# Pivot statistics, output in two halves and another order of work in a cross-attention kernel with a group norm

## What is computed

```
q, k = Wq y + bq, Wk y + bk          # 128 x 1024 each
scores = q k^T / sqrt(128)           # per head, 16 x 16, summed over 1024 positions
attn   = softmax(scores)
o      = Wo (attn (Wv x + bv)) + bo + x
mu, var = mean(o), var(o)            # over all 128 x 1024 values of the batch
out    = (o - mu) * rsqrt(var + 1e-5) * gn_w + gn_b
```

## Time and profile before

| | |
|---|---|
| median of 3 runs | 174.3 us (174.11 to 174.43) |
| the profiled execution | 174.09 us, its span 172.3 us |
| mean granted clock of PE | 0.982 of full speed |
| busy share of the span | PE 94%, DVE 88%, ACT 79%, POOL 65% |
| DMA | 50.8 MB, mean 295 GB/s |

### The profile page before, as it was taken

How to read it: one execution, slowest core, us unless ns; L and a number is a source line. 1 busy time by engine, 2 the same in 40 slices (tenths; PEclk the granted TensorE clock), 3 DMA queues, 4 the chain that set the end, 5 groups by cost and what they waited for, 6 DMA issues and landing times. The chain is left out here.

```text
span 172.3 us, 3697 instructions
## 1 busy us (share of the span) xinstructions
PE 161.3 (94%) x997; PEld 128.1 (74%) x997; DVE 150.8 (88%) x555; ACT 136.7 (79%) x356; POOL 112.5 (65%) x166
## 2 busy tenths in 40 slices
PE   7989999999999999999999999999999999999720
PEld 7777888777777788887777777888877777776410
DVE  1796999999999999999999999999999999977541
ACT  3656588988888888889888888888899888776342
POOL 3287677778777777777787777777777787731010
PEclk9999999999999999999999999999999999999975
DMA  5999778899989999999989999899999865633233
GB/s 198 416 402 372 261 226 305 331 339 327 334 331 345 364 318 332 310 338 335 331 312 338 343 352 359 307 327 337 327 336 332 297 234 230 246 123 124 122 122 122
DMA packets 14276, 50.83 MB, mean 295 GB/s; under 512 B 1712, under 2 KB 1712, under 8 KB 14256
## 3 DMA queue, kind: packets, MB, share of 16 engines
q1 hardware_dynamic: 13968, 50.34, 80.4%
q10 hardware_dynamic: 288, 0.27, 0.5%
HBM read 33.82 MB, written 16.78 MB: 294 GB/s over the span
## 5 line engine op out<-in xcount | busy, mean ns | idle before, releaser
L509 PE MATMUL o_ps<-x_sb,m_sb 128*128 128x512 f32 x128 | 63.0, 614 | 0.0
L426 DVE TENSOR_TENSOR hl_sb<-y_sb,hl_sb 128x512 fp32r<-128x512 f32 x64 | 47.1, 737 | 0.8 <-ACT hl_sb L321 0.8
L266 POOL TENSOR_TENSOR rstd<-veps,nhalf 128x1 f32<-128x1 f32 x32 | 28.3, 885 | 23.2 <-DVE veps L431 23.2
L321 ACT CAST hl_sb<-y_sb 128x512 fp32r<-128x512 f32 x64 | 39.6, 622 | 1.9 <-DMA y_sb<-in_ctx_dram 1.9
L509 PE MATMUL g_ps<-hl_sb 128*128 128x258 f32 x256 | 38.6, 293 | 0.0
L361 ACT ACTIVATE out_sb<-o_ps,shift,gain 128x1024 f32<-128x1024 f32 (+1 forms) x32 | 38.3, 1198 | 0.1
L295 POOL TENSOR_TENSOR lsuma<-hl_sb 128x256 f32<-128x256 f32 x31 | 23.2, 749 | 22.8 <-DVE hl_sb L426 22.8
L509 PEld LDWEIGHTS o_ps<-x_sb,m_sb 128*128 128x128 f32 x128 | 21.8, 191 | 14.8 <-issue 14.8
L509 PEld LDWEIGHTS g_ps<-hl_sb 128*128 128x128 f32 x256 | 32.8, 190 | 0.0
L457 DVE BATCH_NORM_STATS2 bn<-o_ps 128x6 f32<-128x512 f32 x32 | 22.4, 699 | 4.1 <-PE o_ps L509 0.5
L316 ACT ACTIVATE a_sb<-sc_sb,smin 128x128 f32<-128x128 f32 x32 | 12.9, 403 | 16.0 <-DVE smin L417 15.9
(11 more groups left out here) (64 smaller groups left out, 297.8 us busy)
## 6 DMA issues: line engine op xcount, KB each, us to landing
y_sb<-in_ctx_dram SPq DMA_DIRECT2D x32, 512.0 KB, 5.0
x_sb<-in_x_dram SPq DMA_DIRECT2D x32, 512.0 KB, 5.4
out_dram<-out_sb SPq DMA_DIRECT2D x31, 512.0 KB, 4.8
out_dram<-out_sb SPq DMA_DIRECT2D x2, 256.0 KB, 2.2
w_in<-in_weights_dram ACTq DMA_DIRECT2D x1, 256.0 KB, 5.7
cols<-in_columns_dram ACTq DMA_DIRECT2D x1, 3.0 KB, 3.4
```

Of the source, the lines that this page charges most:

```text
L266: nc.gpsimd.tensor_tensor(rstd[:, h1:h1 + 1], veps[:, h1:h1 + 1], nhalf[:, :], ALU.pow).then_inc(rstd_ready, 1)
L321: nc.scalar.copy(hl_sb[:, k, chunks, 0:C], y_sb[:, k, chunks, :]).then_inc(h_ready, 1)
L426: nc.vector.tensor_tensor(hl_sb[:, ky, chunks, C:2 * C], y_sb[:, ky, chunks, :], hl_sb[:, ky, chunks, 0:C].bitcast(F32), ALU.subtract).the ...
L509: return nc.tensor.matmul(dst, lhsT, rhs, start=start, stop=stop, **more)
```

## The change

The pipeline keeps its lags, and nearly every instruction stays. What differs:

- Statistics: the mean with the bias is no longer formed before the product. A pivot (x's first column times the row sums of `m_sb`, plus the bias column; `pivot_column`) is averaged by PE one step ahead, and `shift_by_pivot` gives `cp`. Then the row deviation (`deviation`) and its square plus the variance (`square`) go with the next batch's pivot through one product of three columns (`statistics`), which stands between the two o products and behind the query product of the next step. `negative_variance` and `variance` follow on DVE, then POOL's power as before.
- `fold_matrix` also accumulates the row sums, and the bias column is an instruction of its own.
- PE waits for both halves of the rest before the Gram product starts (in effect one piece).
- The output is written in two halves on ACT, with the copy of the cross product between them.
- Rounding (`round_half`) is one batch ahead: ACT rounds batch t + 1 in step t, and DVE's rests are both of batch t.
- `EARLY` is 2: PE sums the rests of batches 0 and 1 itself, after the transpose. Small matrices get two buffers each. The last batch's o goes to other PSUM banks, and its two halves are stored from ACT and SP.

```diff
+            for t in range(B + LAGS + 1):                 # PE
+                input_product(t - 4, 0)
+                query(t - 2)
+                statistics(t - 5)
+                input_product(t - 4, 1)
+                softmax_product(t - 3)
+                gram(t - 1, 0)
+                gram(t - 1, 1)
+                value_product(t - 3)
+                scores(t - 2)
+                transpose_cross(t - 1)
...
+            for t in range(-1, B + LAGS):                 # ACT
+                normalise(t - 3)
+                round_half(t + 1, 0)
+                scale_bk(t - 2)
+                copy_r(t - 3)
+                gain_and_shift(t - 5)
+                output(t - 5, 0)
+                copy_cross(t - 1)
+                output(t - 5, 1)
+                exponential(t - 2)
+                round_half(t + 1, 1)
...
+            for t in range(B + LAGS + 1):                 # DVE
+                copy_sum(t - 2)
+                invert_sum(t - 3)
...
+                rest_half(t, 0)
+                negative_variance(t - 5)
+                shift_by_pivot(t - 4)
+                variance(t - 5)
+                weighted_shift(t - 5)
+                rest_half(t, 1)
...
+                statistics_of(t - 4, 0)
+                add_query_bias(t - 2)
+                statistics_of(t - 4, 1)
+                fold_matrix(t - 3)
+                aggregate(t - 4)
+                minimum(t - 2)
+                deviation(t - 4)
+                add_gram(t - 1)
+                pivot_column(t - 3)
+                square(t - 4)
...
+            for t in range(B + LAGS):                     # POOL
+                inverse_deviation(t - 5)
+                fold_first(t)
+                fold_last(t - 1)
+                fold_second(t)
+                fold_sum(t)
...
+            def negative_variance(b):
+                dve.wait_ge(st_ready, b + 2)
+                nc.vector.tensor_scalar(nvar[:, b % 2:b % 2 + 1], st_ps[:, 0:1], st_ps[:, 0:1], st_ps[:, 1:2],
+                                        ALU.mult, ALU.add).then_inc(nvar_ready, 1)
+            def variance(b):
+                dve.wait_ge(nvar_ready, b + 1)
+                nc.vector.tensor_scalar(veps[:, b % 2:b % 2 + 1], nvar[:, b % 2:b % 2 + 1], -1.0, EPS,
+                                        ALU.mult, ALU.add).then_inc(veps_ready, 1)
+            def gain_and_shift(b):
+                act.wait_ge(rstd_ready, b + 1)
+                nc.scalar.mul(gain[:, b % 2:b % 2 + 1], gn_w, rstd[:, b % 2:b % 2 + 1])
+                act.wait_ge(wshift_ready, b + 1)
+                nc.scalar.activation(shift[:, b % 2:b % 2 + 1], wshift[:, b % 2:b % 2 + 1], ACT.Identity,
+                                     bias=gn_b, scale=rstd[:, b % 2:b % 2 + 1]).then_inc(affine_ready, 1)
+            def copy_cross(b):
+                act.wait_ge(hl_ready, b + 1)
+                nc.scalar.copy(b2_sb[:, b % 2, :], g_ps[:, C:2 * C]).then_inc(b2_copied, 1)
+            def transpose_cross(b):
+                pe.wait_ge(b2_copied, b + 1)
+                transposed = product(g_ps[:, 0:C], b2_sb[:, b % 2, :], ident_r[:, :], start=False, skip_group_check=True)
+            def statistics(b):
+                if live(b):
+                    pe.wait_ge(q_ready, b + 1)
+                if live(b + 1):
+                    pe.wait_ge(pivot_ready, b + 2)
+                if live(b) or live(b + 1):
+                    part = slice(0 if live(b) else 2, 3 if live(b + 1) else 2)
+                    product(st_ps[:, part], onesn[:, :], st_in[:, b % 2, part]).then_inc(st_ready, 1)
```

More of the change, by code:

```diff
@@ L205, in _ @@
         def _(sp):
[L206 to L220, removed]
-                if is_step(t, LAST):
-                    ko = (k - 5) % UNROLL
-                    for half, done in ((0, normed), (1, normed_dve)):
-                        part = slice(half * HALF, (half + 1) * HALF)
-                        sp.wait_ge(done, B if half == 0 else 1)
-                        sp.dma_start(batch(out, B - 1)[:, part], out_sb[:, ko, part]).then_inc(out_done[ko], 16)
-                elif has(t, 5):
-                    ko = (k - 5) % UNROLL
-                    sp.wait_ge(normed, t - 4)
-                    sp.dma_start(batch(out, t - 5), out_sb[:, ko, :]).then_inc(out_done[ko], 16)
@@ L239, in _ @@
+            for b in range(SLOTS):
+                load_y(b)
+            for t in range(B + LAGS):
+                if t >= 1:
+                    load_y(t + SLOTS - 1)
+                load_x(t)
+                store(t - 5)
+            for k in range(SLOTS):
+                sp.wait_ge(out_done[k], 16 * (B // SLOTS + (k == LAST % SLOTS)))
         @block.gpsimd
@@ new lines, in output @@
+            def output(b, half):
+                if not live(b) or b == LAST and half == 1:
+                    return
+                if b >= SLOTS and half == 0:
+                    act.wait_ge(out_done[b % SLOTS], loads(b - SLOTS))
+                if b == LAST:
+                    act.wait_ge(affine_dve, 1)
+                else:
+                    act.wait_ge(affine_ready, b + 1)
+                k = 2 if b == LAST else b % 2
+                nc.scalar.activation(out_sb[:, b % SLOTS, half_of(half)], o_half(b, half), ACT.Identity,
+                                     bias=shift[:, k:k + 1], scale=gain[:, k:k + 1]).then_inc(normed, 1)
+                if b == LAST:
+                    act.wait_ge(normed, 2 * LAST + 1)
+                    act.dma_start(batch(out, b)[:, half_of(0)], out_sb[:, b % SLOTS, half_of(0)]).then_inc(out_done[b % SLOTS], 16)
@@ L515, in keep_busy, with gram @@
                     product(o_ps[:, 1, 0:P], onesn[:, :], onesn[:, :])
+            def gram(b, half):
+                if not live(b):
+                    return
+                pe.wait_ge(l_ready, 2 * b + 1 + half)
+                if half == 0 and b >= 1:
+                    pe.wait_ge(g_copied, b)
+                    pe.wait_ge(s_copied, b)
+                for c in range(half * HCH, (half + 1) * HCH):
+                    mm = product(g_ps[:, 0:HL], hl_sb[:, b % SLOTS, c, 0:C], hl_sb[:, b % SLOTS, c, :],
+                                 start=(c == 0), stop=(c == CH - 1))
+                if half == 1:
+                    mm.then_inc(hl_ready, 1)
```

659 lines of the change are left out of this document (348 added, 311 removed).

## The result

The changed kernel takes 189.5 us (median of 4 runs, 188.1 to 191.6) against 174.2 us (4 runs, 174.1 to 174.4): 1.085 times as long, 95% interval 1.078 to 1.092. The profiled execution took 190.07 us with a span of 188.0 (before 174.09 and 172.3).

What follows compares the result with a forecast made beforehand. PE set the old 4.74 us step; a ring through power, output, copy and transpose was to make it 5.02. 28 x 0.28 = +7.8, then - 0.1 + 0.4 - 0.6 = +7.5: 181.8 us, range 174.8 to 185.0.

Steps and rivals of the forecast that it cites:

- Is an engine longer than the ring?: Check of each engine's work per step: PE 4.50, ACT 4.59, DVE 4.64 us, POOL unchanged, all below the ring's 5.02.
- the forecast ring: Repeated steps: statistics product, DVE pair, power, gain, shift, first output half, copy, transpose, next o product; 5.02 us a step.
- The start: Up to the first o products of step 4: +0.4 us, bounds -0.3 to +1.9.
- step 4: The step before the ring runs, with no output and set by DVE: about -0.1 us.
- Step 32: Last of the 28 steps in which the ring was to run: +0.28 us.
- The end: Steps 33 and 34 and the last two stores: -0.6 us.
- (1): Rival: the ring is real but shorter, negative_variance 0.16 and power 0.93, step 4.79; 175.4 to 178 us; chance 0.17.
- (2): Rival: power takes 0.55 beside an undelayed rest, ring 4.52, DVE's 4.64 is the step; 171.2 us; chance 0.13.
- (3): Rival: the power gets ahead of the rest and holds it, DVE 4.9 to 5.14; 181.8 to 185.2 us; within forecast's 0.60.
- (4): Rival: second ring through second output half and exponential, 4.93 to 5.15 a step, up to 185.5 us; chance 0.07 with worse.

Runs made afterwards that it cites:

- pointer: The changed kernel with pivot and deviation written as tensor_scalar, their SBUF inputs as pointer operands: 186.9 us, 1.072 of the kernel before.
- early: pointer_copy with statistics first in PE's step, its followers ahead of DVE's rest, pivot and square ahead of add_gram: 207.9 us.
- after: The changed kernel itself, as profiled, no further edit: median 189.5 us, 1.085 of the kernel before.
- copy_first: The changed kernel with ACT's copy of the cross product ahead of the first output half: 188.4 us, 1.081 of the kernel before.
- swap: The changed kernel with the statistics product ahead of the query product on PE: 191.9 us, 1.100 of the kernel before.
- pointer_copy: The changed kernel with both edits, those of pointer and copy_first: 181.8 us, 1.044 of the kernel before.
- rest_late: The changed kernel with DVE's second rest behind the first bn_stats: 197.1 us, 1.124 of the kernel before.
- norm: best with four filling matmuls ahead of the transpose in steps 1 and 2, and ACT's second rounding half moved behind the next normalise: 181.8 us.
- whole: The changed kernel with the output as one instruction again, ahead of the cross product's copy (last batch keeps halves): 199.4 us, 1.145 of the kernel before.
- fill: The changed kernel with two clock-filling matmuls behind the bias rows and in steps 1 and 2: 188.0 us, 1.083 of the kernel before.
- fill6: The changed kernel with six filling matmuls behind the bias rows and in steps 1 and 2: 189.2 us, 1.087 of the kernel before.
- best: pointer_copy with swap, pivot and square ahead of add_gram, weighted_shift behind the second rest, exponential ahead of the second output half: 182.6 us.

## Why the prediction was wrong

**What held.** Direction and mechanism: slower, by a ring that is longer than the old step, with PE waiting at the transpose for ACT's copy (forecast 0.3 to 0.5, seen 0.47). That ring by itself would have made the step 5.14, as pointer shows. Its terms came out close:

| term | predicted | measured |
|---|---|---|
| o to query | 0.90 | 0.94 |
| query to statistics | 0.22 | 0.22 |
| to veps, two links | 0.73 | 0.43 + 0.38 |
| veps to power | 0.24 | 0.23 |
| power, to gain, to shift | 1.05 + 0.03 + 0.19 | 1.10 + 0.03 + 0.20 |
| shift to output | 0.41 | 0.47 |
| output to copy, copy, to transpose | 0.68 + 0.27 + 0.05 | 0.68 + 0.26 + 0.04 |
| transpose to o | 0.25 | 0.24 |
| sum | 5.02 | 5.22 |

negative_variance took 0.27, as assumed; its dependent veps starts 0.38 after it instead of 0.31: shift_by_pivot (cp) stands between the two, which the forecast left out, and veps starts 0.04 after its end (88.17 + 0.14 = 88.31). The product's 0.43 isn't its own length: negative_variance starts at 87.97, 0.15 after the product's end at 87.82, since DVE's rest runs to 88.04 (instructions overlap by some 0.07). In the rows of pointer and early the waiting one starts 0.04 after the product's end (90.39 + 0.28, 90.71; 95.33 + 0.38, 95.75); on a free DVE the link is thus 0.28 + 0.04 = 0.32. With 0.32 the ring of after is 5.11, an estimate; pointer measures 5.14, so its own length is 0.09 to 0.12 above the sum.

**What failed.** The step "Is an engine longer than the ring?" and the rivals behind it. It looked at sums of busy time for POOL ("POOL does the same work as before"), gave the pivot 0.13 us without asking what runs on POOL beside it, and listed for a second ring only that through the exponential. The binding one goes through POOL's own queue: the power stands ahead of four folds, and the pivot and the deviation, which have two SBUF inputs, didn't end before a fold that had begun ahead of them. What I had used for the rest and the power held for the pivot too. This ring's terms give 5.23; pointer (step 5.14), copy_first (5.22), swap (5.22) and pointer_copy (4.95) tell it apart from the forecast ring. So the step's 0.20 above the forecast is 0.09 to 0.12 for small terms of the sum and 0.11 to 0.08 for the missed ring, 27 times: 5.4 of the 6.1 us by which these steps exceed the forecast. The other 0.65 is two steps that took 5.60 and 5.49; in the first veps starts 0.42 late behind nothing that the profile names. The first of them (step 14) comes in the same place in most kernels of the new order (5.60 in copy_first, 5.50 in pointer, 5.30 in pointer_copy) and not before the change (4.73), so it belongs to the program and isn't noise. Its cause stays open.

The Trainium skill ("SBUF — State Buffer", "two separate sides") says that the DVE and GpSimd port pair is locked for a whole operation, and that the second to come waits. The traces agree where DVE's rest came first (power 0.93) and where a fold did (rest 1.20 in rest_late), and show more than I had used it for: also a 128x1 operation is held, 0.73 us in copy_first against 0.27 with pointers. They don't agree where the power came first; the two rows behind the forecast both had the rest first and didn't test that order. In after the power starts up to 0.01 us ahead of the rest in nearly every step and is still drawn out to 1.10; in norm it starts 0.07 to 0.13 ahead and the rest isn't held at all (0.69). Here the measurement decides: beside a rest the power's length goes by their distance, and no run shows a rest held by it.

**The start** was the other half of the miss: +3.1 instead of +0.4. PE stands idle 1.32 us before the first transpose (8.21); its granted clock is 1.00 until 10 us, 0.50 from 11 to 16, and full again from 18. With the same start at full clock (whole) step 4's o product comes at 16.73: 1.0 us is the order, where I had 0.4, and 2.1 the clock. It isn't fixed in the code: after and whole have the same start, PE idle 1.32 and 1.48 us before that transpose, and the clock was 0.50 in the one and 1.00 in the other. In fill PE was idle only 0.66 us there, and the clock fell too; what decides it stays open. The runs of after agree with this: at mean clocks of 0.991, 0.982, 0.974 and 0.957 they took 188.1, 189.0, 190.1 and 191.6 us, while those of fill6, all at 0.991 or 0.992, spread over 0.4. The forecast took full clock for granted, as the rows of the kernel before show it in the steps; the start's own clock I had not weighed.

**Step 32** took no more than before: no rest is made in it, the power takes 0.55, and the ring is short. It counts as 27 steps, not 28. **The end** (-0.9 for -0.6) and **step 4** were right in sign and near in size.

**Rivals.** (1), the shorter ring, fell: the power took 1.10. (2) fell: the step would have been under 4.74. What it supposed, that both get by, does happen, but only with the power 0.07 us or more ahead of the rest, in norm (0.55 and 0.69). (3) didn't come up in this order, and no run shows it: in norm the power was ahead and the rest ran in its usual time; what held the rest in rest_late was a fold. (4) isn't the ring of after, but stood right behind: with both others shortened it sets pointer_copy's 4.95 (forecast for it 4.93).

**What is the new order's own cost?** Of the 0.48 us that a step lost, 0.33 comes back by reordering and pointers (5.22 to 4.89). The remaining 0.15 stays: DVE is busy 4.68 us a step in best, against 77.11 us of the 80 from 60 to 140, 4.57 a step, before the change. With 0.2 us of room in a step of 4.89 a wait that one moves off DVE's path easily comes back elsewhere, as in norm. DVE's 4.68 is near the forecast's sum of 4.64 for its work. Whether some order reaches 4.74 isn't settled; none of those tried did, and none beats the kernel before.

## What to carry to other kernels

When an order written by hand is changed in a kernel whose engines are all near 90%, list every ring through every queue, those of the engine that looks idle too: POOL was busy 59% of the span and was in the ring that decided. For each DVE operation that moves, look at which GpSimd operation it now falls beside; with two SBUF tensors it cost what was left of a fold, however few elements it had, and pointer operands avoided this. If two rings are about equally long, undoing one shows little or nothing: try the edits together before dropping either.

## What the runs showed of the hardware

- A 128x1 `scalar_tensor_tensor` with two SBUF tensors took 0.21 us with POOL idle, 0.37 with a fold under way, 0.73 when it began with the fold (after, copy_first); as `tensor_scalar` with pointers 0.26 to 0.27 in every case (pointer, pointer_copy, best). A 128x1 `tensor_tensor` took 0.15 alone, 0.24 when a fold had 0.23 left (after) and 0.49 when it had 0.48 left (rest_late), with a pointer 0.21.
- The power takes 0.55 us alone, 0.93 when a rest began 0.16 ahead, 1.10 when it began 0.01 behind, and 0.55 again when it began 0.07 to 0.13 behind (norm), the rest then taking its usual 0.69. A rest that began 0.10 behind a fold took 1.20.
- PE's clock at the start differed between executions with the same start (0.50 in after and 1.00 in whole from 12 to 16 us), and is worth 2.1 us here.
